# Macaron layer on eight cores: Wq tiles of the next head staged ahead of the output projection, RoPE of the queries in halves

## What is computed

```python
x = x + 0.5 * ffn(layernorm(x))       # base linear 4096x4096 + gated LoRA experts
x = x + attn(layernorm(x))
x = x + 0.5 * ffn(layernorm(x))

def attn(x, Wq, Wk, Wv, Wo):          # H = 32 heads of 128, one K and one V head
    Q, K, V = x @ Wq.T, x @ Wk.T, x @ Wv.T
    Qr = Q * cos + rotate_half(Q) * sin          # RoPE, also for K
    # windows of 512 keys at steps of 256; sigmoid scores, divided by their sum,
    # overlapping windows are blended linearly
    return concat_heads(out) @ Wo.T
```

## Time and profile before

| | |
|---|---|
| time, median of 2 runs | 4755.84 us (4751.14 to 4760.53) |
| profiled execution, its own time | 4524.91 us |
| its span, slowest core (core 0) | 4523.3 us |
| spans of the 8 cores | 4496.9 to 4523.3 us |
| TensorE matmul busy | 3104.1 us, 69% of the span |
| VectorE busy | 995.7 us, 22% |
| ACT busy | 1324.4 us, 29% |
| GpSimd busy | 533.3 us, 12% |
| attention heads, groups 0 to 3 | from about 1331 to 3564 us, with three Wo stages in between |
| Wo stages | from 1707.8, 2322.1, 2940.0 and 3565.8 us |

### The profile page before, as it was taken

One profiled execution on the slowest core, in us unless ns is written; L12 is line 12 of the kernel. 1 busy time (PEld: TensorE's weight loads), 2 busy tenths in 40 slices (PEclk: granted clock), 3 DMA queues, 4 the chain that ended last, 5 costly groups with the idle time before them and its releaser, 6 DMA issues.

```text
span 4523.3 us, 41117 instructions; the slowest of 8 cores (4496.9 to 4523.3 us)
## 1 busy us (share of the span) xinstructions
PE 3104.1 (69%) x14804; PEld 1481.6 (33%) x14804; DVE 995.7 (22%) x1698; ACT 1324.4 (29%) x2047; POOL 533.3 (12%) x772
## 2 busy tenths in 40 slices
PE   2549999994366666566656666666666563459998
PEld 1224444442223332233332233322333221224443
DVE  3441111115712220013210032200232100441111
ACT  3332211114423323233323333232333232432221
POOL 1101111111111112200012100022000121001111
PEclk8669999997678778888878888788888787669999
DMA  4325566554453437831138611077311387337875
GB/s 133 93 58 168 168 179 175 168 154 123 118 159 112 129 95 133 142 84 47 47 65 143 128 38 56 19 140 140 74 50 44 64 145 142 90 107 216 223 216 169
DMA packets 647226, 537.40 MB, mean 119 GB/s; under 512 B 33905, under 2 KB 566642, under 8 KB 646770
## 3 DMA queue, kind: packets, MB, share of 16 engines
q0 software_dynamic: 90112, 251.71, 24.2%
q1 hardware_dynamic: 556914, 283.07, 23.8%
HBM read 408.85 MB, written 125.83 MB: 118 GB/s over the span
## 4 chain that ended last, share of the span: by engine, by line
PE 49%; DMA 23%; DVE 12%; ACT 8%; issue 5%; DVEq 1%; SPq 1%; POOL 0%; ACTq 0%; POOLq 0%
PE PS L443 20%; PE PS L606 8%; DMA x2h<-arena 7%; PE PS L758 6%; DMA arena<-wqT 4%; ACT arena L275 4%; DMA arena<-woT 4%; PE PS L690 3%; PE PS L671 3%; DMA arena<-x2h 2%; DVE arena L250 2%; DMA out<-arena 2%; DVE arena L254 2%; DVE arena L699 2%; DVE arena L710 2%
## 5 line engine op out<-in xcount | busy, mean ns | idle before, releaser
L443 PE MATMUL PS<-arena 128*128 128x512 bf16 x5120 | 1135.9, 380 | 25.5 <-ACT arena L275 15.8
L275 ACT ACTIVATE arena<-arena 128x512 bf16<-128x512 f32 (+1 forms) x784 | 567.6, 762 | 1060.6 <-PE PS L446 600.7
L758 PE MATMUL PS<-arena 128*128 128x512 bf16 x2048 | 590.5, 453 | 356.0 <-ACT arena L275 356.0
L443 PEld LDWEIGHTS PS<-arena 128*128 128x128 bf16 x5120 | 501.8, 98 | 634.3 <-issue 34.6
L606 PE MATMUL PS<-arena 128*128 128x512 bf16 x2048 | 586.3, 428 | 20.9 <-ACT arena L275 20.9
L758 PEld LDWEIGHTS PS<-arena 128*128 128x128 bf16 x2048 | 221.1, 112 | 724.7 <-issue 585.6
L46 POOL DMA_DIRECT2D x2h<-arena x256 | 217.2, 849 | 1886.5 <-ACT arena L766 1629.7
L671 PE MATMUL PS<-arena 128*128 128x512 bf16 (+1 forms) x640 | 195.7, 379 | 237.9 <-ACT arena L675 128.4
L675 ACT ACTIVATE arena<-PS 128x512 bf16<-128x512 f32 (+1 forms) x640 | 292.2, 509 | 225.2 <-PE PS L671 224.4
L766 ACT ACTIVATE arena<-PS 128x512 f32<-128x512 f32 x256 | 152.8, 597 | 664.5 <-PE PS L758 403.8
L699 DVE COPY arena<-PS 128x516 f32<-128x516 f32 (+1 forms) x160 | 94.1, 588 | 985.7 <-PE PS L690 985.7
(11 more groups left out here) (99 smaller groups left out, 2098.0 us busy)
## 6 DMA issues: line engine op xcount, KB each, us to landing
arena<-wbaseT SPq DMA_DIRECT2D x256, 512.0 KB, 6.5
x2h<-arena POOLq DMA_DIRECT2D x320, 256.0 KB, 5.0
arena<-wqT SPq DMA_DIRECT2D x256, 256.0 KB, 3.4
arena<-woT SPq DMA_DIRECT2D x256, 256.0 KB, 5.6
arena<-xin POOLq DMA_DIRECT2D x24, 1024.0 KB, 9.5
arena<-xin POOLq DMA_DIRECT2D x96, 256.0 KB, 4.7
x1h<-arena POOLq DMA_DIRECT2D x96, 256.0 KB, 2.3
arena<-x1h POOLq DMA_DIRECT2D x24, 1024.0 KB, 9.0
```

The source lines that it names most:

```text
L275: c = pr.emit("scalar", lambda s, si=i % nb, d=dst_bf_ap: s.activation(d, wstage[si], ACT.Copy), wc, 1)
L443: pr.emit("tensor", lambda t, c=c, sl=slot, of=of, t0=t0, n=n: t.matmul(sl, wb[of % 2][:, c, :], xlnb[:, c, t0:t0 + n], start=(c == 0), st ...
L758: mmc = pr.emit("tensor", lambda t, gg=gg, of=of, ts2=ts2, sl=slot: t.matmul(sl[:, 0:512], wqb[of % 2][:, gg, :], wout8[:, gg, ts2 * 512:( ...
```

## The change

Three edits. `qt1` and `qt2`, the work areas of RoPE, shrink from 1024 to 512 words each, and RoPE of a head runs as two halves of 512 columns, with a drain between the halves: eight VectorE operations in place of four. The room goes to `wob`, two weight buffers of 8 blocks that only the output projection uses; `wqb` is then free during it. And `stage_wq` for the next group's first head moves from behind the Wo loop to ahead of it, no longer waiting for that loop's last matmul; the 64 Q matmuls stay behind the loop.

```diff
-        qt1 = a.f32(1024)
-        qt2 = a.f32(1024)
+        qt1 = a.f32(512)
+        qt2 = a.f32(512)
         qrb = [a.bf16(1024), a.bf16(1024)]
+        wob = [a.bf16(8 * 128, (8, 128)), a.bf16(8 * 128, (8, 128))]
...
-                pr.emit("vector", lambda v, par=par: v.tensor_tensor(
-                    qt1, PS1[:, 0:1024], cosx[:, 256:1280], ALU.mult), [("tensor", qmm[h])], 1)
-                pr.emit("vector", lambda v: v.tensor_tensor(qt2[0:64, :], PS1[64:128, 0:1024],
-                                                            s2x[0:64, 256:1280], ALU.mult), [], 1)
...
-                pr.drain()
-                rope[h] = pr.emit("vector", lambda v, par=par: v.tensor_tensor(
-                    qrb[par], qt1, qt2, ALU.add), [], 1)
+                for hf in range(2):
+                    if hf == 1:
+                        pr.drain()
+                    pr.emit("vector", lambda v, hf=hf: v.tensor_tensor(
+                        qt1, PS1[:, hf * 512:(hf + 1) * 512],
+                        cosx[:, 256 + hf * 512:768 + hf * 512], ALU.mult),
+                        [("tensor", qmm[h])] if hf == 0 else [], 1)
...
+                    pr.drain()
+                    rope[h] = pr.emit("vector", lambda v, par=par, hf=hf: v.tensor_tensor(
+                        qrb[par][:, hf * 512:(hf + 1) * 512], qt1, qt2, ALU.add), [], 1)
...
+            if hp < 3:
+                stage_wq(hp * 8 + 8, extra=[("tensor", womm_prev_grp)])
+                nxfeed = make_qfeeder(hp * 8 + 8)
+            else:
+                nxfeed = lambda k: None
             for of in range(NIF):
...
-                          wqb[of % 2][:, s2_ * 4:(s2_ + 1) * 4, :], (), ew)
+                          wob[of % 2][:, s2_ * 4:(s2_ + 1) * 4, :], (), ew)
...
-                            sl[:, 0:512], wqb[of % 2][:, gg, :],
+                            sl[:, 0:512], wob[of % 2][:, gg, :],
...
-            if hp < 3:
-                stage_wq(hp * 8 + 8, extra=[("tensor", womm_last)])
-                feed = make_qfeeder(hp * 8 + 8, extra_first=[("scalar", wo_ev[63])])
-                feed(64)
+            nxfeed(64)
```

More of the change, by code:

```diff
@@ L622, in attn @@
                 par = h % 2
-                pr.emit("vector", lambda v, par=par: v.tensor_tensor(
-                    qt1, PS1[:, 0:1024], cosx[:, 256:1280], ALU.mult), [("tensor", qmm[h])], 1)
-                pr.emit("vector", lambda v: v.tensor_tensor(qt2[0:64, :], PS1[64:128, 0:1024],
-                                                            s2x[0:64, 256:1280], ALU.mult), [], 1)
-                pr.emit("vector", lambda v: v.tensor_tensor(qt2[64:128, :], PS1[0:64, 0:1024],
-                                                            s2x[64:128, 256:1280], ALU.mult), [], 1)
-                pr.drain()
-                rope[h] = pr.emit("vector", lambda v, par=par: v.tensor_tensor(
-                    qrb[par], qt1, qt2, ALU.add), [], 1)
+                for hf in range(2):
[5 more added lines that the diff above has]
+                        [("tensor", qmm[h])] if hf == 0 else [], 1)
+                    pr.emit("vector", lambda v, hf=hf: v.tensor_tensor(
+                        qt2[0:64, :], PS1[64:128, hf * 512:(hf + 1) * 512],
+                        s2x[0:64, 256 + hf * 512:768 + hf * 512], ALU.mult), [], 1)
+                    pr.emit("vector", lambda v, hf=hf: v.tensor_tensor(
+                        qt2[64:128, :], PS1[0:64, hf * 512:(hf + 1) * 512],
+                        s2x[64:128, 256 + hf * 512:768 + hf * 512], ALU.mult), [], 1)
+                    pr.drain()
+                    rope[h] = pr.emit("vector", lambda v, par=par, hf=hf: v.tensor_tensor(
+                        qrb[par][:, hf * 512:(hf + 1) * 512], qt1, qt2, ALU.add), [], 1)
                 if hh < 7:
```

## The result

The changed kernel takes 1.006 times the time of the kernel before, 95% interval 1.0040 to 1.0081: slower by 18 to 37 us of some 4550. Its median over 27 executions is 4579.47 us, that of the kernel before, over the 26 that now stand beside it, 4624.93 us. The ratio is not that of these medians: in part of the executions, with either kernel, the cores of one die or of both run at a lower granted clock (0.74 to 0.83 where the others have 0.84) and take up to 350 us longer, the two that stood for the kernel before when the prediction was made (4751 and 4761 us) among them, and every ratio here leaves such executions out.

A forecast was written before the change was run, and what follows sets the result against it. TensorE was taken to have the chain's largest share; the change was read only at Wo's start and end and RoPE. 31.8 - 19.5 + 6.8 = +19.1 us on the 4755.84 us median gave 4775 us, range 4745 to 4808.

The forecast's parts named there:

- rival A: At the Wo starts, early Wq loads and casts are covered in head 7 and cost nothing: -12.7 us, 4743 us; chance 5%.
- Start of Wo: At three Wo starts the first matmul waits for ten casts, 11.9 us in place of 1.28: 31.8 us slower in all.
- the bounds of 12.5 and 43.8: Limits in us for the three Wo starts: no cast waiting for a DMA, or loads slowed by accumulating stores.
- the quiet row: Mid-group cast timing, rounds of 3.64 and 3.72 us, taken for Wo starts because no stores run there yet; gives 31.8 us.
- Q projection: Behind Wo at three boundaries, 64 matmuls run without waiting for casts, 14.81 us from last eviction to RoPE: 19.5 us gained.
- RoPE: Halves take 5.90 us in place of 5.05; 0.85 us more counts in each group's first and last head: 6.8 us.
- the second part of QK in the 24 middle heads: In middle heads it still waits for the sigmoid queued behind the casts, so RoPE's extra 0.85 us disappears there.
- Clock at the start of Wo: First 16 Wo matmuls already run at the 1.2 GHz level, 6.37 us, so the longer gap adds nothing.
- the rule about the idle stretch: An idle TensorE restarts at half clock; by it each of three Wo starts would cost about 2.8 us more.
- B: RoPE's extra time counts in every head, 20.4 us above the forecast sum: +39.5 us, 4795 us; chance 8%.
- C: Unbroken Q projection behind Wo runs at 1.2 GHz, 27.5 us in place of 14.0: +59.7 us, 4815 us; chance 7%.
- D: Wo loop falls into its long form, every group 8.19 us in place of 7.34: +128 us, 4884 us; chance 3%.

The follow-up runs named there:

- the second run: Changed kernel with Wq staging still moved ahead of Wo but RoPE whole as before; ratio to the kernel before 1.0045.
- the first and third run: Kernel before with only RoPE changed: in halves, ratio 1.0034; in four parts of 256 columns, ratio 0.9998.

## Why the prediction was right or wrong

The forecast was +19.1 us on 4755.84, or a ratio of 1.004; the measured ratio is 1.006, 1.0040 to 1.0081. The sign, the mechanism and nearly the size were right, but the predicted time of 4775 us lies 196 us above the measured median of 4579.47, and the range of 4745 to 4808 lies wholly above it. The step that failed is the base of the sum: "I work the sum out on the profiled execution and add it to the median". That median, 4755.84, was of two executions, 5.1% above the profiled one; the median of 26 is 4624.93, and their lowest is 4514.58. The prediction noted the 231 us and did not ask what they were; it only asked whether they would stretch the terms. On the profiled execution's 4524.91 the same sum is 4544, where the profiled execution after took 4554.08. With a gap twelve times as large as the effect, the range should have reached down to the profiled time. Its lower end of 4745 also lay just above the 4743 of the prediction's own rival A.

The terms, one by one:

- Start of Wo: forecast 3 x 10.6 = 31.8 us, measured 34.1, +11.3 at each. The tenth cast started 12.8 us after the first on core 0 (1720.46 to 1733.29) and 11.9 on average, not 11.1; the bounds of 12.5 and 43.8 held. The reason to take the quiet row was right.
- Q projection: forecast 19.5 us, measured 17.6. On core 0 the 64 matmuls took 13.97 us, the figure worked out. Over the cores the means from last eviction to RoPE are 15.25, 15.03 and 15.45 us, up to 0.6 us above the 14.81 foreseen; and core 0, from which the time before was read, had the longest of the three old stretches at the third boundary (24.05 us, mean of the cores 21.76).
- RoPE: forecast 0.85 us in 8 heads, 6.8 us. RoPE took 5.92 us, as worked out (5.90), and QK came 0.87 us later in both, 7.0 us: the term was right. The heads as a whole do not show it as cleanly. In the changed kernel the first heads are 0.75 us longer, the last 1.44, the middle ones 0.17 shorter, 4.5 us in all; with RoPE as before (the second run) it is +0.5, +0.4 and +0.35, with quarters the part of the last head behind RoPE is not longer than before (37.98 us, 37.90 before). So the 0.6 us by which the last heads exceed 0.87 are not shown to be RoPE's. That the second part of QK in the 24 middle heads comes no later held in the changed kernel (10.41 us, 10.44 before) and within 0.3 us in every run with three buffers.
- Clock at the start of Wo: nothing added; the first 16 matmuls took 5.33 us after the gap of 13.98 us, where they took 6.37; over eight cores and the three places the means are 6.2 to 6.6 us now and 6.7 to 6.8 before. So the rule about the idle stretch cost nothing here, as the row had it.
- The sum of these, with the 4.5 us that the heads as a whole are longer, is 34.1 - 17.6 + 4.5 = 21 us at the end of attention on the mean core, against 19.1. That it comes so near is partly luck, since the heads differ by more than that between runs without a cause. The rest of the 30 us of the two profiled executions is the second FFN, which differs by 17 us between two runs of one kernel.

Rival A was excluded for the right reason: ACT's order. B fell by the first and third run. C did not happen. D did not happen: the Wo stages are 935 us with either start.

## What to carry to other kernels

A stage moved ahead of another in an in-order queue is not hidden unless the queue has slots to run ahead with: with three staging buffers, seven of the ten tiles that the first Wo matmul had to wait for were loaded in the open. Before splitting an operation whose wait is on record, look at what ends last behind that wait; here the wait of a 108.8 us row could grow by 0.9 us a head and cost nothing in 24 of 32 heads, and the buffers in front of the sigmoid were worth 115 us. And when the times shown and the profiled execution differ by many times the effect, forecast a ratio from the profile and let the range reach down to it.

## What the runs showed that was not expected

With more delay on VectorE the middle heads were faster. With RoPE 2.7 us later, TensorE's second wait fell from 4.2 to 1.7 us on average, the six matmuls after it from 2.74 to 2.10 us, and a kernel with 384 more VectorE instructions ran at 0.9998 of the time. The mean granted clock of the span was 0.845, against 0.843 in the kernel before and 0.837 in the changed one. Splitting one idle stretch of TensorE differently moved some of its work between the 1.2 and the 2.4 GHz level in this run; how the two waits must lie for that was not shown.

A DMA from DRAM to DRAM was harmless here when spread and harmful in a bunch: eight of 2 MB at once held back 256 KB loads to 59 us, and one in each head of 41 us was not seen in the length of the heads.
